# Feed-forward layers on fp16 parts instead of fp32r parts in an attention and FFN kernel

## The chip, the cores and the metric

The kernel runs on one core of one Trainium2 chip. The metric is the device time of one execution in microseconds; the time before is the median of three runs, and one further execution was profiled. Engines are named as in the profile: PE (TensorE, matmuls), PEld (its weight loads), DVE (VectorE), ACT (ScalarE), POOL (GpSimd), SP (SyncE, which only issues DMAs here).

## What is computed

8192 tokens of width 128 go through an attention over 4096 stored keys and values, a residual and a layer norm, then a gated feed-forward network of hidden width 512, a residual and a second layer norm. Everything is fp32.

```python
q = hidden @ Wq.T + bq                            # (8192, 128)
scores = q @ memory_keys.T / sqrt(128)            # (8192, 4096)
mem_out = softmax(scores) @ memory_values
x = layernorm(hidden + mem_out @ Wo.T + bo)

_tlin = lambda x, w, s: einsum('bsi,oi->bso', x, w) * s
h = silu(_tlin(x, w1_w, w1_s)) * _tlin(x, w2_w, w2_s)      # 128 -> 512, twice
h = gelu(_tlin(h, h1_w, h1_s), approximate=False)          # 512 -> 512
h = gelu(_tlin(h, h2_w, h2_s), approximate=False)          # 512 -> 512
out = layernorm(x + _tlin(h, w3_w, w3_s))                  # 512 -> 128
```

The FFN's weight matrices hold -8, 0 and 8 only; their columns' scales are arbitrary fp32 numbers. The kernel finds out on the chip whether the weights are exact in its short format, and has a second path for those that are not.

## The kernel before

**Short formats.** fp32 operands are split into a high part in the format of the matmul and a low part, the rest; a product is then the sum of two or three matmuls in that format. The attention's scores and the whole FFN use fp32r (32 bits wide), probabilities and values use fp16.

**Attention stage** (the first 740 us). Tokens are worked on in 32 pairs of 128-token tiles. One frame (`frame(f, par)` on every engine) has 16 steps t and scores pair f while it ends the softmax of pair f-1 and multiplies the values of pair f-2. TensorE computes three matmuls a step for the scores (L1043 to L1045) and the four of a value step (L1017 to L1022); the values of a pair follow 16 steps behind. VectorE moves each quarter of the scores out of PSUM and takes its maximum (L828), ends each tile with the maximum and the bias of exp (L834, L836), and turns pieces of 32x32 (L795). ScalarE takes exp of a piece at every even step (L629; tile 0 begins at t = 8, right behind the high part of the next q, L608) and makes the fp16 high part of one value step in each t (`high_part`, L638). GpSimd makes the low part behind it (L549). SyncE sends each turned piece with four DMAs (`exchange`, `send`, L380) into one of two buffers `slot_p`, in the order of the pieces; the first send of a pair waits until GpSimd has done the pair before last (`split`).

**The weight check.** In frames 3 to 27 a piece of 226 columns of the packed FFN weights is loaded on ScalarE's queue (t = 3), copied to fp32r (t = 13), subtracted by GpSimd (L555, t = 15), and VectorE reduces the rest's absolute value in the next frame, behind the bias of tile 0 (j = 3, L850). A last maximum, turned on TensorE, gives `low_max`: if it is zero the low parts of the weights are left out.

**The passage** (about 690 to 780 us). `last_values` on TensorE does the values of pairs 30 and 31 with the first layer of block 0 in between (behind value step 8 of pair 30), then h1 of block 0. GpSimd makes the low parts of pair 30 up to step 11, VectorE the later ones and all of pair 31. VectorE also splits x1 of block 0 there (`split_x1(dve, 0)`).

**Feed-forward stage.** 16 blocks of 512 tokens. A turn i (`turn(i, i2, par)`) does on TensorE, in this order: first layer of block i+1 (w1 and w2, 4 chunks, 16 matmuls; chunks 2 and 3 wait for the gate and the product to leave their banks), h2 of block i (32 matmuls, bank j waits for gate or product of block i+1 to leave), h1 of block i+1 (32; behind its chunk 0 the turning of x1 of block i+2), w3 of block i (8). The four banks of `ring` are shared by all. ScalarE: table of Silu, two gates, two high parts, two gates, table of Gelu, two high parts, then for each chunk of h2 and of h1 a Gelu into `gelu` and a second Gelu into `h_hi` (L715, L719). VectorE: products and their low parts, residual and moments of block i+2, its normalisation to x1 (L190), the norm of block i-1, the low parts of h2's Gelus (L895), two of h1's, the split of x1, the last two of h1's. GpSimd: `add_bias` (L158) and `inverse_deviation` (L164, L167), whose rstd VectorE's normalisation waits for. In turn 0 the add for block 3 follows right behind the rstd of block 2.

The order of ScalarE's work at h1's end:

```python
for j in chunks:
    act.wait_ge(done, 4 * b + j + 1)
    at_least(act, gelu_split[layer - 1], 4 * b + j - 3)
    nc.scalar.activation(gelu[:, layer - 1, j, :], ring[:, j, :], ACT.Gelu, ...).then_inc(gelu_f[layer - 1], 1)
    if j == 0:
        at_least(act, *used_by)
    nc.scalar.activation(h_hi[layer][:, j, :], ring[:, j, :], ACT.Gelu, ...).then_inc(gelu_h[layer - 1], 1)
```

## Time and profile before

| | us |
|---|---|
| median of 3 runs | 1117.59 (1116.14 to 1117.80) |
| profiled execution | 1117.46 |
| its span | 1115.50 |
| PE busy | 1079.3 (97%) |
| DVE busy | 972.2 (87%) |
| ACT busy | 903.1 (81%) |
| POOL busy | 643.0 (58%) |
| DMA queue of the sends | 58.7% of 16 engines' time |

The span is what the profiler sees from the first to the last instruction; the rest of the execution's time lies around it. A matmul's busy time is modelled and overlaps its neighbour's: an engine at 97% tells that it hardly stands still, and only the distance from one start to the next tells its pace. In the timelines a row is start, duration, engine, line, operation, output and inputs, shapes, a count of merged instructions, and in brackets the idle time before it with what ended it.

### The profile page before, as it was taken

Reading aid. Unit: us, or ns where it says so; the run is one execution under the profiler, and the core shown is the slowest. Engines: PE = TensorE matmul, PEld = TensorE weight load, DVE = VectorE, ACT = ScalarE, POOL = GpSimd, SP = SyncE. Lnnn points to the kernel's source line nnn. Section 1 sums busy time; section 2 is a strip of 40 time slices with the busy share of each in tenths; the row PEclk is TensorE's granted clock in tenths of the full one; section 3 lists DMA queues with packets and bytes.
Section 4 is the critical chain, followed back from the end, with each engine's and each line's share of the span. In section 5 each row is a group of like instructions: output and inputs, shape, how many; then the busy total and the mean of one; then the engine's idle time right before and its main releaser. Section 6 shows DMA issues by size and latency. Waiting matters only on the chain.

```text
span 1115.5 us, 20017 instructions
## 1 busy us (share of the span) xinstructions
PE 1079.3 (97%) x5324; PEld 770.6 (69%) x5324; DVE 972.2 (87%) x1806; ACT 903.1 (81%) x1609; POOL 643.0 (58%) x617
## 2 busy tenths in 40 slices
PE   6899999999999999999999999979999999999996
PEld 5666666666666666666666666646888888888875
DVE  6999999999999999999999899897888887888884
ACT  6787788878887888888878878788788888888883
POOL 0487888888888888888888888760211211121111
PEclk9999999999999999999999999999999999999998
DMA  6879888988988889888888998891010010011000
GB/s 202 203 185 212 198 201 210 209 200 202 209 203 206 203 207 210 200 202 209 206 203 204 212 200 188 193 255 55 12 46 28 28 56 28 28 35 50 11 13 27
DMA packets 83957, 165.89 MB, mean 149 GB/s; under 512 B 19664, under 2 KB 47824, under 8 KB 83792
## 3 DMA queue, kind: packets, MB, share of 16 engines
q1 hardware_dynamic: 71536, 154.29, 58.7%
q10 hardware_dynamic: 12384, 11.16, 3.5%
q8 instruction: 18, 0.29, 0.1%
q14 instruction: 19, 0.16, 0.0%
HBM read 22.76 MB, written 8.39 MB: 28 GB/s over the span
## 4 chain that ended last, share of the span: by engine, by line
PE 42%; SPq 13%; issue 11%; POOL 10%; ACT 10%; DMA 6%; DVE 5%; ACTq 1%; POOLq 0%; DVEq 0%
PE ring L1090 13%; SPq L380 12%; PE ring L1091 12%; POOL pT L549 10%; DMA slot_p<-rows 6%; ACT rows L629 5%; ACT pT L638 4%; PE o_ps L1017 2%; PE s_ps L1045 2%; PE s_ps L1043 2%; PE s_ps L1044 2%; PE o_ps L1020 2%; PE o_ps L1022 2%; DVE rows L795 2%; DVE rows L828 1%
## 5 line engine op out<-in xcount | busy, mean ns | idle before, releaser
L549 POOL TENSOR_TENSOR pT<-slot_p,pT 128x512 f16<-128x512 f32 x482 | 546.0, 1167 | 124.4 <-ACT pT L638 124.3
L638 ACT ACTIVATE pT<-slot_p 128x512 f16<-128x512 f32 x512 | 296.5, 617 | 73.8 <-DMA slot_p<-rows 68.6
L828 DVE TENSOR_SCALAR_CACHE_REDUCE rows<-s_ps 128x1024 f32<-128x1024 f32 x256 | 309.4, 1209 | 40.5 <-DMA slot_p<-rows 19.9
L795 DVE STREAM_TRANSPOSE rows<-rows 128x1024 f32<-128x1024 f32 x256 | 316.9, 1239 | 5.9 <-issue 4.1
L629 ACT ACTIVATE rows<-rows,bias 128x1024 f32<-128x1024 f32 x256 | 291.6, 1139 | 6.4 <-DVE bias L836 5.9
L1043 PE MATMUL s_ps<-keys,q_buf 128*128 128x512 f32 x512 | 249.2, 487 | 6.8 <-DVE rows L828 3.5
L1017 PE MATMUL o_ps<-pT,v_hi 128*128 128x512 f16 x512 | 197.4, 385 | 13.3 <-POOL pT L549 6.6
L1045 PE MATMUL s_ps<-keys,q_buf 128*128 128x512 f32 x512 | 202.4, 395 | 0.0
L1044 PE MATMUL s_ps<-keys,q_buf 128*128 128x512 f32 x512 | 201.1, 393 | 0.0
L1020 PE MATMUL o_ps<-pT,v_lo 128*128 128x256 f16 x1024 | 196.1, 273 | 0.0
L1022 PE MATMUL o_ps<-pT,v_hi 128*128 128x512 f16 x512 | 194.6, 380 | 0.0
L164 POOL TENSOR_TENSOR var_eps<-moments,eps 128x4 f32<-128x4 f32 x31 | 6.2, 200 | 297.6 <-DVE moments L185 297.6
L1020 PEld LDWEIGHTS o_ps<-pT,v_lo 128*128 128x128 f16 x1024 | 101.1, 99 | 85.4 <-issue 0.6
L1090 PE MATMUL ring<-keys,w_all 128*128 128x512 f32 x384 | 153.4, 400 | 1.0 <-ACT gate L690 0.9
L1091 PE MATMUL ring<-keys,w_all 128*128 128x512 f32 x384 | 150.5, 392 | 0.0
L715 ACT ACTIVATE gelu<-ring,scales 128x512 f32<-128x512 f32 x128 | 87.8, 686 | 57.8 <-PE ring L1091 57.8
L1017 PEld LDWEIGHTS o_ps<-pT,v_hi 128*128 128x128 f16 x512 | 49.3, 96 | 100.0 <-issue 46.8
L1043 PEld LDWEIGHTS s_ps<-keys,q_buf 128*128 128x128 f32 x512 | 96.8, 189 | 25.7 <-DVE rows L828 4.9
L1045 PEld LDWEIGHTS s_ps<-keys,q_buf 128*128 128x128 f32 x512 | 96.1, 188 | 22.5
L1044 PEld LDWEIGHTS s_ps<-keys,q_buf 128*128 128x128 f32 x512 | 96.8, 189 | 17.3
L895 DVE TENSOR_TENSOR h_lo<-gelu,h_hi 128x512 fp32r<-128x512 f32 x128 | 81.9, 686 | 25.5 <-ACT h_hi L719 25.4
L1090 PE MATMUL ring<-h_hi,w_all 128*128 128x512 f32 x256 | 103.1, 403 | 0.3 <-ACT gate L690 0.3
(110 smaller groups left out, 1329.2 us busy)
## 6 DMA issues: line engine op xcount, KB each, us to landing
slot_p<-rows SPq DMA_DIRECT2D x1024, 128.0 KB, 3.0
x_in<-in_x SPq DMA_DIRECT2D x16, 256.0 KB, 3.4
x_in<-in_xT ACTq DMA_DIRECT2D x30, 128.0 KB, 3.3
out<-y_out SPq DMA_DIRECT2D x15, 256.0 KB, 2.4
o_scratch<-o_sum ACTq DMA_DIRECT2D x29, 128.0 KB, 2.7
o_in<-o_scratch SPq DMA_DIRECT2D x14, 256.0 KB, 3.1
z<-in_w_all ACTq DMA_DIRECT2D x25, 113.0 KB, 2.7
rows<-in_w_all SPq DMA_DIRECT2D x1, 2816.0 KB, 12.1
```

The lines of the kernel that those rows point to most:

```text
L549: nc.gpsimd.tensor_tensor(halves(s % RING, 1), slots_first(pp, s), halves(s % RING, 0), ALU.subtract).then_inc(split, 1)
L629: nc.scalar.activation(s, s, ACT.Exp, bias=bias[:, tile:tile + 1], scale=SCALE, accum_out=den[:, bass.ds((2 * p + tile) * PIECES + k, 1)]) ...
L638: nc.scalar.activation(halves(s % RING, 0), slots_first(pp, s), ACT.Copy).then_inc(highed, 1)
L795: nc.vector.transpose(row_piece(tile, k), row_piece(tile, k)).then_inc(turned, 1)
L828: nc.vector.tensor_scalar(row_piece(tile, k), s_ps[:, j % 2, :], 1.0, None, ALU.mult, ALU.max, accum_out=part_max[:, tile, k:k + 1]).then_ ...
L1017: nc.tensor.matmul(o_ps[:, pp, :], v_hi[:, 2 * s, :], pT[:, s % RING, 0, :], start=s == 0, stop=False, skip_group_check=True)
L1020: nc.tensor.matmul(o_ps[:, pp, 0:2 * P], v_lo[:, 2 * s + c, :], pT[:, s % RING, c, 0:2 * P], start=False, stop=False, skip_group_check=True)
L1043: nc.tensor.matmul(out, q_h, k_h, start=True, stop=False)
L1044: nc.tensor.matmul(out, q_h, k_l, start=False, stop=False)
L1045: last = nc.tensor.matmul(out, q_l, k_h, start=False, stop=True)
L1090: nc.tensor.matmul(out, wh, hh, start=n == 0, stop=False)
L1091: last = nc.tensor.matmul(out, wh, hl, start=False, stop=final and not low_weights)
```

## The change

- The first three FFN layers (w1 and w2, h1, h2) multiply fp16 high and low parts with fp16 weights; w3 stays fp32r, with a copy of its weights made on ScalarE. The number of matmuls is the same.
- To stay in fp16's range, h is scaled by powers of two. They come from bounds that are found on the chip: the largest weight of each layer and the largest scale (`find_maxima`, `turn_maxima`, `spread_maxima`, `share_maxima`, `keep_maxima`, `set_scales`).
- h1's high part is no longer a second Gelu from PSUM but a Copy of the first one, scaled (`gelu_high`), and it is queued one chunk behind the Gelus; the low part is a fused multiply and subtract. TensorE's first layer and h2's bank now wait for the first Gelu (`gelu_f`), not for the high part.
- The check takes 256 columns a frame instead of 226. VectorE reduces rest and weights in one instruction (512 columns) at j = 2 instead of j = 3; the load is issued at t = 9 instead of t = 3.
- Inexact weights no longer get low parts: the raw weights are kept in fp32, and whole fp32 matmuls are run. h2's raw weights are scaled by GpSimd in turn 0, on either path. Their load waits for the last scores instead of the last sends.

The diff, cut to its core:

```diff
-CHECK_COLS = 226
+CHECK_COLS = 256
-        self.w_all = sb("w_all", [P, CHECK_COLS * CHECKS], FP32R)
+        self.w_all = sb("w_all", [P, CHECK_COLS * CHECKS], FP16)
+        self.w3_hi = sb("w3_hi", [P, HC * P], FP32R)
...
+    def find_maxima(self, dve, parts):
+        by_chunk = parts[:, :].rearrange("p (c n) -> p n c", n=2)
+        self.nc.vector.reduce_max(self.found[:, 0:1], by_chunk[:, 1, :], AX.X).then_inc(self.found_ready, 1)
...
+    def spread_maxima(self, dve):
+        dve.wait_ge(self.found_turned, 1)
+        self.nc.vector.reduce_max(self.low_max[:, :], self.x1_ps[0:FOUND, 2 * P:3 * P], AX.X).then_inc(self.low_found, 1)
+        dve.wait_ge(self.low_found, 1)
+        self.nc.vector.tensor_scalar(self.spread[:, :], self.ident[0:FOUND, :], 0.0, self.low_max[:, :], ALU.mult, ALU.add).then_inc(self.low_spread, 1)
...
+    def set_scales(self, dve):
+        dve.wait_ge(self.bounding, 1)
+        self.nc.vector.tensor_tensor(self.sizes[:, :], self.maxima[:, 1:4], self.maxima[:, 4:7], ALU.mult).then_inc(self.bounding, 1)
+        dve.wait_ge(self.bounding, 2)
+        self.nc.vector.tensor_scalar(self.bounds[:, 0:1], self.sizes[:, 0:1], self.sizes[:, 1:2], LEAST, ALU.mult, ALU.max).then_inc(self.bounding, 1)
...
+        self.nc.vector.tensor_scalar(self.powers[:, :].bitcast(I32), self.bounds[:, :].bitcast(I32), EXPONENT, None,
+                                     ALU.bitwise_and).then_inc(self.bounding, 1)
+        dve.wait_ge(self.bounding, 5)
+        self.nc.vector.reciprocal(self.inverses[:, :], self.powers[:, :]).then_inc(self.bounding, 1)
+        dve.wait_ge(self.bounding, 6)
+        for col, by, factor in ((HC, self.inverses[:, 0:1], 1.0), (2 * HC, self.powers[:, 0:1], 1.0), (3 * HC, self.powers[:, 1:2], 2.0 ** 9)):
+            self.nc.vector.tensor_scalar(self.scales[:, col:col + HC], self.scales[:, col:col + HC], by, factor,
+                                         ALU.mult, ALU.mult).then_inc(self.scales_set, 1)
...
-        for tile in range(2):
-            for k in range(PIECES):
-                sp.wait_ge(sent[tile][k], 16 * GROUPS * PAIRS)
+        sp.wait_ge(scored, 8 * PAIRS)
         sp.dma_start(raw, w_raw[:, 0:W_COLS]).then_inc(raw_loaded, 16)
...
         def turn(i, i2, par):
             if valid(i + 2, BLOCKS):
                 stage.add_bias(pool, i + 2, i2 + 1, par)
                 stage.inverse_deviation(pool, i + 2, 0)
+            if is_step(i, 0):
+                pool.wait_ge(raw_loaded, 16)
+                pool.wait_ge(stage.scales_set, 4)
+                nc.gpsimd.tensor_tensor(raw_h2, raw_h2, stage.h1_scale[:, :].broadcast_to([P, HC * HID]), ALU.mult).then_inc(raw_scaled, 1)
...
-                if t == 3 and checking(f):
-                    at_least(act, w_rested, f - FIRST_CHECK)
+                if t == 9 and checking(f):
+                    at_least(act, w_maxed, f - FIRST_CHECK)
                     act.dma_start(w_check, w_raw[:, bass.ds((f - FIRST_CHECK) * CHECK_COLS, CHECK_COLS)]).then_inc(check_loaded, 16)
...
+        def gelu_high(b, j):
+            act.wait_ge(gelu_f[0], 4 * b + j + 1)
+            nc.scalar.activation(h_hi[1][:, j, :], gelu[:, 0, j, :], ACT.Copy, scale=stage.h1_scale[:, :]).then_inc(gelu_h[0], 1)
...
             if valid(i + 1, BLOCKS):
-                gelus(i + 1, 1, mid1_done, (mid2_done, 4 * (i + 1)), (1, 2, 3))
+                gelu_high(i + 1, 0)
+                for j in (1, 2, 3):
+                    mid1_of(i + 1, j)
+                    if j >= 2:
+                        gelu_high(i + 1, j - 1)
+                gelu_high(i + 1, 3)
...
+        nc.scalar.activation(stage.w3_hi[:, :], stage.w_all[:, W_AT["w3"]:W_COLS], ACT.Copy).then_inc(stage.w3_ready, 1)
...
-                if j == 3 and checking(f - 1):
+                if j == 2 and checking(f - 1):
                     dve.wait_ge(w_rested, f - FIRST_CHECK)
-                    nc.vector.reduce_max(low_parts[:, bass.ds(f - FIRST_CHECK - 1, 1)], w_rest, AX.X,
+                    nc.vector.reduce_max(low_parts[:, bass.ds((f - FIRST_CHECK - 1) * 2, 2)],
+                                         check_room.rearrange("p (n c) -> p n c", n=2), AX.X,
                                          apply_absolute_value=True).then_inc(w_maxed, 1)
...
+            if layer == 1:
+                nc.vector.scalar_tensor_tensor(out=h_lo[1][:, j, :], in0=gelu[:, 0, j, :], scalar=stage.h1_scale[:, :],
+                                               in1=h_hi[1][:, j, :], op0=ALU.mult, op1=ALU.subtract).then_inc(gelu_split[0], 1)
...
         stage.output_sum(dve, PAIRS - 3, 1)
+        stage.set_scales(dve)
         stage.split_x1(dve, 0)
```

## Rows read from the trace of the kernel before

**Rows 1.** Busy us (x instructions) of PE, PEld, DVE, ACT, POOL; PEclk, DMA, GB/s.
```profile
100.00:700.00 600.00, 595.99 (x3059) 400.89 (x3058) 554.42 (x848) 497.38 (x933) 502.56 (x458) 1.00 0.88 204
790.00:1100.00 310.00, 309.07 (x1418) 250.68 (x1418) 251.06 (x680) 254.71 (x409) 49.44 (x68) 1.00 0.10 31
```
**Rows 2.** Timeline of ACT in one turn: start us, duration, instruction, [idle before <-releaser].
```profile
876.88 0.69 ACT L715 ACTIVATE gelu<-ring,scales 128x512 f32<-128x512 f32 x1 [0.54 <-PE ring L1091]
878.16 1.28 ACT L684 ACT_TABLE_LOAD   x1
885.02 1.14 ACT L698 ACTIVATE keys<-gate 128x512 fp32r<-128x512 f32 x2
886.07 0.67 ACT L715 ACTIVATE gelu<-ring,scales 128x512 f32<-128x512 f32 x1
...
898.62 0.69 ACT L715 ACTIVATE gelu<-ring,scales 128x512 f32<-128x512 f32 x1 [0.54 <-PE ring L1091]
```
**Rows 3.** Waits of SyncE's queue in 100 to 700 us: total, times, longest.
```profile
SPq L380 <- POOL pT L549: 39.9, 24, 2.2
```
**Rows 4.** Timelines of DVE, ACT, POOL and PE in frames 18 and 19.
```profile
420.82 0.39 DVE L850 TENSOR_REDUCE low_parts<-z 128x226 f32 x1
442.97 0.39 DVE L850 TENSOR_REDUCE low_parts<-z 128x226 f32 x1
421.03 1.15 ACT L629 ACTIVATE rows<-rows,bias 128x1024 f32<-128x1024 f32 x1
443.60 1.14 ACT L629 ACTIVATE rows<-rows,bias 128x1024 f32<-128x1024 f32 x1
409.59 1.17 POOL L549 TENSOR_TENSOR pT<-slot_p,pT 128x512 f16<-128x512 f32 x1 [0.50 <-ACT pT L638]
411.16 0.38 PE L1017 MATMUL o_ps<-pT,v_hi 128*128 128x512 f16 x1
433.62 0.10 PEld L1017 LDWEIGHTS o_ps<-pT,v_hi 128*128 128x128 f16 x1 [0.61 <-POOL pT L549]
```
**Rows 5.** Timeline of PE in the attention stage, one period of two steps.
```profile
401.22 0.40 PE L1044 MATMUL s_ps<-keys,q_buf 128*128 128x512 f32 x1
...
402.38 0.39 PE L1017 MATMUL o_ps<-pT,v_hi 128*128 128x512 f16 x1
...
403.92 0.40 PE L1044 MATMUL s_ps<-keys,q_buf 128*128 128x512 f32 x1
```
**Rows 6.** Timelines of ACT and PE in turn 0: last Gelu of h1, start of h2.
```profile
767.98 0.69 ACT L715 ACTIVATE gelu<-ring,scales 128x512 f32<-128x512 f32 x1 [0.55 <-PE ring L1091]
774.08 0.50 PE L1090 MATMUL ring<-h_hi,w_all 128*128 128x512 f32 x1 [0.25 <-ACT gate L690]
```
**Rows 7.** Timeline of PE in the turn of rows 2: start of h2, turning of x1.
```profile
883.08 0.50 PE L1090 MATMUL ring<-h_hi,w_all 128*128 128x512 f32 x1
...
892.51 0.27 PE L231 MATMUL x_ps<-ident,x 128*128 128x128 f32 x1
```
**Rows 8.** Timelines of DVE, POOL and PE around x1, in a full turn and in turn 0.
```profile
890.81 1.12 DVE L190 TENSOR_SCALAR x<-z,moments,rstd 128x128 f32<-128x128 f32 x4 [0.29 <-POOL rstd L167]
781.68 1.30 POOL L158 TENSOR_TENSOR xb<-x_in,bo_all 128x512 f32<-128x512 f32 x1
781.81 1.25 DVE L190 TENSOR_SCALAR x<-z,moments,rstd 128x128 f32<-128x128 f32 x1 [1.48 <-POOL rstd L167]
782.98 0.85 DVE L190 TENSOR_SCALAR x<-z,moments,rstd 128x128 f32<-128x128 f32 x3
783.88 0.33 PE L231 MATMUL x_ps<-ident,x 128*128 128x128 f32 x1 [0.24 <-DVE x L190]
```
**Rows 9.** Groups by line, 100 to 700 us: busy us, mean ns | idle before.
```profile
L549 POOL TENSOR_TENSOR pT<-slot_p,pT 128x512 f16<-128x512 f32 x430 | 487.0, 1167 | 96.9 <-ACT pT L638 96.9
...
L836 DVE TENSOR_SCALAR bias<-row_max 128x1 f32<-128x1 f32 x53 | 8.2, 154 | 1.8
```
**Rows 10.** Timeline of POOL in the passage, beside the same subtraction on DVE.
```profile
738.32 1.61 POOL L568 TENSOR_TENSOR pT<-slot_p,pT 128x512 f16<-128x512 f32 x1
```

More of the change, by code:

```diff
@@ L769, in _ @@
         stage.output_half(act, PAIRS - 1, 1)
-        gelus(0, 1, mid1_done, (mid2_done, 0))
+        act.wait_ge(stage.scales_set, 4)
+        for j in range(HC):
+            mid1_of(0, j)
+            gelu_high(0, j)
         turns(act, turn)
@@ L1079, in frame, with split_products @@
                     stage.turn_x1(pe, 0)
         frames(pe, frame)
[L1083 to L1086 removed]
+        def split_products(out, pairs, sem_done, parts_ready=None):
+            for n, (w, hh, hl) in enumerate(pairs):
                 if parts_ready:
                     pe.wait_ge(parts_ready[0], parts_ready[1] + n + 1)
[L1089 to L1094 removed]
@@ L1096, in layer @@
-        def layer(out, name, j, src, sem_done, low_weights, width=HID, parts_ready=None):
-            split_products(out, [(weight(name, k, j, width), weight_low(name, k, j, width),
-                                  h_hi[src][:, k, :], h_lo[src][:, k, :]) for k in range(HC)], sem_done, low_weights,
-                           parts_ready if j == 0 else None)
+                nc.tensor.matmul(out, w, hh, start=n == 0, stop=False)
+                last = nc.tensor.matmul(out, w, hl, start=False, stop=n == len(pairs) - 1)
@@ new lines, in split_products, with whole_products, layer @@
+            last.then_inc(sem_done, 1)
+        def whole_products(out, pairs, sem_done, parts_ready=None):
+            for n, (w, h) in enumerate(pairs):
+                if parts_ready:
+                    pe.wait_ge(parts_ready[0], parts_ready[1] + n + 1)
+                last = nc.tensor.matmul(out, w, h, start=n == 0, stop=n == len(pairs) - 1)
+            last.then_inc(sem_done, 1)
+        def layer(out, b, name, j, src, sem_done, low_weights, width=HID, parts_ready=None):
+            parts_ready = parts_ready if j == 0 else None
+            if low_weights:
+                whole_products(out, [(raw_weight(name, k, j, width), gelu[:, src - 1, k, :] if src else product(b, k))
+                                     for k in range(HC)], sem_done, parts_ready)
+            else:
+                split_products(out, [(weight(name, k, j, width), h_hi[src][:, k, :], h_lo[src][:, k, :])
+                                     for k in range(HC)], sem_done, parts_ready)
```

185 lines of the change are left out of this document (102 added, 83 removed).

## Prediction

> **What bounds the kernel now.** I read the busy time by stage first. In the attention stage TensorE is busy 596 of 600 us, in the feed-forward stage 309 of 310 us, always at the full clock [rows 1]; those busy times are modelled ends, so next comes the spacing of the matmuls and what is late next. In the feed-forward stage a turn (one block of 512 tokens) takes 21.74 us, from the last Gelu behind h1 to the same one a turn later [rows 2]. TensorE hardly waits there, so only its pace counts, until another chain becomes longer. In the attention stage a second loop is as long: ScalarE's exp, GpSimd's low parts, SyncE's sends (which wait for GpSimd 24 times in 27 frames [rows 3]), and back to TensorE, which is found waiting 0.61 us for GpSimd at the start of a pair [rows 4].
>
> **1. The pace of a matmul.** Six fp32r matmuls and six equivalents in fp16 take 2.70 us; five intervals of fp32r take 1.16 us, 0.232 each, which leaves 0.218 for fp16 [rows 5]. So fp16 is worth 0.014 us on each 512-column matmul. A block has 88; the 8 of w3 stay fp32r. 80 x 0.014 = 1.1 us a block, 18 us in 16 blocks, if TensorE stays the limit. The number of matmuls is unchanged.
>
> **2. ScalarE behind the last h1 product.** Before, two operations stand between the end of h1's chunk 3 and the loading of the Silu table, both Gelus (876.88 to 878.16, 1.28 us) [rows 2]. After, there are three: the Gelu, the high part of chunk 2 (now queued behind it), the high part of chunk 3. The extra one is a Copy from SBUF; two of them take 1.05 us before the next operation starts, 0.52 each [rows 2], and the last one is a little shorter than a Gelu: +0.46. Behind it are queued the table, the gates (on which VectorE's products wait, and h2 on TensorE, which needs gate 2 to leave bank 0), and the second pair of high parts, on which VectorE's low parts and then the normalised x1 wait. What this chain takes is seen in turn 0, where TensorE does wait for it: 774.08 - 767.98 = 6.10 us from Gelu to h2 [rows 6]; in a full turn it is 883.08 - 876.88 = 6.20 [rows 2, 7]. So it has 0.10 us of slack. New: 6.56.
> From h2's start 40 matmuls (h2 and h1's first chunk) come in 40 x 0.218 = 8.72 us: 15.28 after the Gelu. There TensorE turns x1, which VectorE finishes at 890.81 + 1.12 = 891.93, 15.05 after the Gelu [rows 8]; with ScalarE's 0.46 and a signal of 0.05 that is 15.56, the later of the two. From the turning to the next last Gelu it was 898.62 - 892.51 = 6.11 [rows 2, 7], now less 24 x 0.014: 5.77. Sum 21.33 against 21.74: 0.4 us a turn instead of 1.1. Over the 14 full turns -5.6 us. Bounds: 0 (a Copy scaled from a register column as slow as a Gelu, and a late split of x1) and -1.1 a turn. VectorE's fused low part of h1 may cost 0.06 more than the plain subtraction, four times a turn; it fits in VectorE's idle fifth [rows 1]. In the last turn the extra operation and the two fused ones delay z2 by some 0.8 where h2 gains 0.45; block 0 gains 0.3 in h1. These cancel.
>
> **3. The weights of h2, scaled on GpSimd in turn 0.** This runs whatever the weights are. It has 2048 columns: four times the add of 512 columns there is 5.2 us [rows 8], four times the subtraction to fp16 4.7 [rows 9]; I take 4.7. It is issued right behind the rstd of block 2, on which VectorE's x1 waits too. The trace shows what comes of that: at 781.68 GpSimd's add starts, at 781.81 VectorE's first normalisation, which takes 1.25 us where the next three take 0.85 together, and its successor starts at 782.98, when GpSimd is done; TensorE waits for x1 then [rows 8]. Such operations take turns and do not overlap: where both engines subtract back to back GpSimd's last 1.61 instead of 1.17 us [rows 9, 10]. So with the scaling in that place VectorE's first slice ends at about 786.7, then the add takes its turn (some 1.1) before the other three slices (0.85): x1 is ready at about 788.5 instead of 783.83. That is +4.7 on TensorE, which has no slack there; less 0.3 of faster h1: +4.4. Bounds: 0 (VectorE gets in first) and +5.5.
>
> **4. The weight check in the attention loop.** The reduction grows from 226 to 512 columns: 0.39 us [rows 4] for 226, by the same rate at most 0.88, by one column a ns 0.68; I take 0.64 in sequence. It moves from behind the bias of tile 0 to before chunk 3 of it, so that bias comes 0.64 later. The slack of bias to the exp that reads it is about 0.2 us in one frame (the reduction behind it starts at 420.82, exp at 421.03) and 0.6 in the next (442.97, 443.60) [rows 4]; exp is late by 0.45 and by 0 to 0.1 in turn. Queued behind it on ScalarE are the high parts of the last steps of a pair, which release GpSimd's, which release the sends of the next pair, which run back to back and let TensorE's values start. This loop spans two frames. The one that holds TensorE back (0.61) is that with little delay; in the other GpSimd ends at 409.59 + 1.17 = 410.76 what TensorE starts at 411.16 [rows 4], 0.4 of slack for 0.45 of delay. So some 0.15 per two frames, and up to 0.07 a frame for GpSimd's 256 columns instead of 226: 0.08 to 0.15 a frame, +2.0 us over 25 frames with what is passed on. Bounds: 0, and 0.54 per two frames, +6.8. The load at step 9 instead of 3 has four steps to land, 5.4 us by [rows 5]; a transfer of its size needs some 3 us of them, so nothing.
> In the last frames exp waits for the bias itself, so the last wide reduction, the four small maxima and the spreading of the maxima pass through: +0.5, +0.4, +0.3, together +1.2 (0 to +3), estimates from the 0.39 us reduction and the 0.154 us operation [rows 4, 9].
>
> **5. set_scales.** Ten small VectorE operations ahead of the split of x1, 0.154 us each [rows 9] and about 0.04 for the signal: 1.9 us. TensorE's first layer follows some 3 us behind the old split, and GpSimd keeps TensorE back later: hidden. But GpSimd subtracts back to back there. If the five of more than one column each have to let it pass, 1.1 us apiece, the split comes about 3 us too late, of which some 1 is absorbed: +2.2. Bounds 0 and +3; I take +1.5. The Trainium skill (VectorE: DVE Perf Modes, section on mode 2×_2P) lets single-source fp32 operations in SBUF take both read ports if their outer dimension is even, which four columns are and one is not. Here one column ran in 0.154 us beside a busy GpSimd; for four no row shows it; by the page this term would be 2.2 and the sum 1121.7.
> The copy of w3 on ScalarE (+0.6) lies in ScalarE's wait for the first layer. The raw load, now issued without waiting for the sends to land, keeps its place in SyncE's queue, and nobody reads it before turn 0.
>
> **Sum.** Profiled run 1117.46 us (span 1115.50 and 1.96 around it; the median is 1117.59): -5.6 + 4.4 + 2.0 + 1.2 + 1.5 = +3.5, so 1121.0, own range 1117.5 to 1125.
>
> **Rivals.** (a) TensorE's pace decides: the extra Copy and x1 find slack that I do not see, all 18 us come, less parts 3 to 5 (9.1): 1108.5. Against it: turn 0, where the chain is seen at 6.10. Chance 0.12. (b) The long scaling costs nothing (VectorE gets in first, or GpSimd takes it in pieces): 1116.6. Against it: the slice of 1.25 us. 0.20. (c) Slower: the exp delay decides the attention loop. Place: the bias of tile 0 in frames 3 to 27; price 0.54 us per two frames; it decides as soon as the delayed loop has no slack left, which I put at 0.4: +6.8 instead of 2.0, and the last frames and set_scales at their upper ends (+3.3): 1129. For it: TensorE waits for GpSimd now. 0.15. (d) The change does not do what it says: the weights are found inexact and whole fp32 matmuls run. Their values are 0 and 8 in size and exact in fp16, so 0.02; the time would be far above the range. My forecast keeps 0.51.
>
> **Chances.** A measurement can tell about 0.2%, 2.2 us, from no change. Slower by more (over 1119.8): 0.68 of the forecast, (c), (d): 0.52. Within: 0.3 of the forecast and most of (b): 0.27. Faster: (a), a third of (b): 0.21. The range that leaves 2 in 10 out is 1111 to 1128; it holds cases of both signs, and the likeliest one's own is 1117.5 to 1125.
>
> **What would show it.** Turns of 21.3 us, fp16 matmuls at 0.218, the table load 1.74 us behind the last h1 Gelu, and TensorE waiting for gate 2 and for x1: part 2. Turns of 20.6: (a). A GpSimd operation of over 4 us in turn 0 and a VectorE slice as long beside it: part 3. Longer waits of TensorE for GpSimd at a pair's start: part 4, and (c) if every second frame grows by half a us. A split of x1 that TensorE waits for: part 5. I am wrong if x1's chain is not the later one in a turn, or if exp waits for bias in neither frame.

## The result, and the profile after

| | before | after |
|---|---|---|
| median us | 1116.88 (1116.14 to 1117.80, 4 runs) | 1129.51 (1129.19 to 1129.69, 4 runs) |
| ratio, 95% interval | | 1.0112 (1.0095 to 1.0130) |
| span of the profiled execution | 1115.5 | 1127.4 |

The change makes the kernel slower by 12.6 us. The sign was forecast, the size was not: 1121.0 was said, with 1111 to 1128 as the range, and the time is 1.5 us above it.

I cut both spans at operations of ScalarE that both kernels have: the copy of the last q (in the middle of frame 30), the load of the Gelu table behind the gates in turn 0, and the same in turn 1. Timeline of ScalarE, after (start us, duration, instruction, idle before and what ended it):

```profile
695.84 0.48 ACT L664 ACTIVATE q_buf<-x_ps,bq_col 128x256 fp32r<-128x256 f32 x1 [1.21 <-PE x_ps L1077]
...
783.62 1.28 ACT L740 ACT_TABLE_LOAD   x1
...
810.98 1.28 ACT L740 ACT_TABLE_LOAD   x1
```

Before, these stood at 689.93, 774.62 and 796.67. So:

| stretch | before | after | difference | forecast |
|---|---|---|---|---|
| attention, to the last q | 689.93 | 695.84 | +5.9 | +2.9 (part 4) |
| passage, to the table load of turn 0 | 84.69 | 87.78 | +3.1 | +1.8 (part 5, and 0.3 of part 4) |
| turn 0 to turn 1 | 22.05 | 27.36 | +5.3 | +4.4 (part 3) |
| the rest | 318.83 | 316.42 | -2.4 | -5.6 (part 2) |
| sum | 1115.50 | 1127.40 | +11.9 | +3.5 |

The 0.3 is the spreading of the maxima, which stands behind the last q (716.81 to 723.19). No stretch has the wrong sign, and all four miss in the same direction. Each column is one profile. Three more profiles with this same attention stage were taken in the experiments; their last q stands at 696.49, 697.61 and 697.88, so the stage lost between 5.9 and 8.0 us, and differences of 1 or 2 us in it are told by medians only.

Busy time by stage, answering [rows 1]; the columns are those of rows 1:

```profile
100.00:700.00 600.00, 592.01 (x3033) 397.46 (x3032) 550.98 (x843) 494.05 (x927) 498.36 (x454) 1.00 0.87 203
790.00:1100.00 310.00, 299.67 (x1407) 146.26 (x1406) 257.12 (x675) 256.27 (x409) 53.50 (x69) 0.99 0.10 30
```

The fp16 weight loads show at once (PEld 146 us instead of 251). They overlap the matmuls in both kernels; whether part of the shorter spacing is theirs, no run tells. TensorE's busy time fell by 9.4 us in the feed-forward stage and by 4 in the attention stage, where nothing of its work was changed. There it stood still, which is what a lower busy time means on the engine that sets the pace.

**A turn.** Timelines of ScalarE and TensorE in a full turn, answering [rows 2, 7, 8]:

```profile
884.18 0.66 PE L296 MATMUL x_ps<-ident,x 128*128 128x128 f32 x4
890.06 0.69 ACT L772 ACTIVATE gelu<-ring,scales 128x512 f32<-128x512 f32 x1 [0.43 <-PE ring L1172]
890.64 1.32 ACT L778 ACTIVATE h_hi<-gelu,h_scale 128x512 f16<-128x512 f32 x2
891.99 1.28 ACT L740 ACT_TABLE_LOAD   x1
```

The table load comes 1.93 us behind the last Gelu of h1, where it came 1.28 behind it [rows 2] and 1.74 was forecast. The two scaled Copies take 1.32 together and 0.71 singly, the plain ones 1.14 together [rows 2] and 0.62 singly; the estimate counted 0.52 for the extra one, half of the 1.05 from the start of two plain ones to the next operation. Turns take 21.61 us.

**Turn 0.** Timelines of GpSimd, VectorE and TensorE, answering the last four of [rows 8]:

```profile
789.68 1.02 POOL L180 TENSOR_TENSOR rstd<-var_eps,minus_half 128x4 f32<-128x4 f32 x1
790.67 3.60 POOL L644 TENSOR_TENSOR raw<-raw,h_scale 128x2048 f32<-128x2048 f32 x1
794.23 1.26 POOL L171 TENSOR_TENSOR xb<-x_in,bo_all 128x512 f32<-128x512 f32 x1
790.80 5.28 DVE L203 TENSOR_SCALAR x<-z,moments,rstd 128x128 f32<-128x128 f32 x4 [1.48 <-POOL rstd L180]
796.14 0.66 PE L296 MATMUL x_ps<-ident,x 128*128 128x128 f32 x4 [4.25 <-DVE x L203]
796.92 0.63 PE L1172 MATMUL ring<-in_room,w_all 128*128 128x512 f16 x1
...
799.48 0.63 PE L1172 MATMUL ring<-in_room,w_all 128*128 128x512 f16 x1
...
800.26 0.38 PE L1172 MATMUL ring<-in_room,w_all 128*128 128x512 f16 x1
```

The slices of x1 stand behind the scaling and then behind the add, as forecast; TensorE waits 4.25 us. What was not forecast is behind it: the seven matmuls from 796.92 to 799.48 start 0.43 us apart, not 0.22. The granted clock of the stretch says why (0.72 is the mean of stretches at half and at the full level, that is 1.2 and 2.4 GHz), with the stretch behind it:

```profile
795.00:801.00 6.00, 4.86 (x17) 2.15 (x18) 4.15 (x8) 1.89 (x3) 0.48 (x1) 0.72 0.00 0
801.00:811.00 10.00, 9.75 (x48) 5.13 (x47) 6.45 (x10) 8.28 (x14) 0.00 (x0) 1.00 0.00 1
```

**The passage.** Timelines of VectorE and TensorE; the forecast had no row for the operations on four columns beside a busy GpSimd. There are nine operations (the prediction counted ten):

```profile
740.49 0.75 DVE L269 TENSOR_TENSOR sizes<-maxima 128x3 f32<-128x3 f32 x1
741.27 0.21 DVE L271 TENSOR_SCALAR bounds<-sizes 128x1 f32<-128x1 f32 x1
...
741.77 0.58 DVE L275 TENSOR_SCALAR powers<-bounds 128x2 int32<-128x2 int32 x1
742.39 0.17 DVE L278 RECIPROCAL inverses<-powers 128x2 f32<-128x2 f32 x1
742.59 0.88 DVE L281 TENSOR_SCALAR scales<-scales,inverses 128x4 f32<-128x4 f32 x1
743.38 2.30 DVE L281 TENSOR_SCALAR scales<-scales,powers 128x4 f32<-128x4 f32 x2
745.60 0.14 DVE L283 TENSOR_SCALAR h_scale<-inverses 128x1 f32<-128x1 f32 x1
745.66 1.39 DVE L229 CAST x_hi<-rows 128x512 f16<-128x512 f32 x1
747.92 0.38 PE L1171 MATMUL ring<-x_hi,w_all 128*128 128x512 f16 x1 [3.59 <-DVE x_lo L231]
```

The nine take 5.2 us (740.49 to 745.66), five of them more than half a microsecond, and TensorE waits 3.59 us for the split of x1. Its first matmuls behind the wait still come at full pace; from 749.00 to 752.41 they are at half the clock again.

**The attention loop.** ScalarE's exp waits for the bias hardly at all: the waits of 100 to 690 us, answering [rows 3, 4] (engine, line, waited for: us in total, times, longest):

```profile
ACT pT L694 <- DMA slot_p<-rows: 60.1, 25, 3.1
...
PE o_ps L1098 <- POOL pT L611: 7.9, 15, 0.7
...
ACT rows L685 <- DVE bias L911: 2.0, 3, 0.9
```

The same of the kernel before:

```profile
ACT pT L638 <- DMA slot_p<-rows: 59.4, 26, 3.2
...
PE o_ps L1017 <- POOL pT L549: 3.2, 10, 0.6
```

TensorE waits for GpSimd at a pair's start 7.9 us, before 3.2. The frames are longer by nearly what rival (c) had said, but its mechanism, exp behind a late bias, isn't there. The experiments had to find what is.

### The profile page after: what moved, and what is told of

It is laid out like the page before. It is cut to its first block, busy times and chain, and to the rows that moved or that the text cites. A ratio compares the mean times of both kernels' runs of the same rounds, so it can differ in the third digit from the quotient of the medians.

```text
span 1127.4 us, 20029 instructions
## 1 busy us (share of the span) xinstructions
PE 1073.1 (95%) x5326; PEld 656.6 (58%) x5326; DVE 981.8 (87%) x1820; ACT 907.2 (80%) x1610; POOL 645.2 (57%) x617
## 4 chain that ended last, share of the span: by engine, by line
issue 33%; PE 20%; POOL 18%; ACT 9%; DVE 7%; SPq 6%; DMA 4%; ACTq 0%; POOLq 0%; DVEq 0%
POOL pT L611 15%; SPq L446 5%; DMA slot_p<-rows 4%; ACT rows L685 3%; ACT pT L694 3%; PE ring L1171 3%; PE ring L1172 2%; PE o_ps L1098 2%; PE s_ps L1126 2%; PE s_ps L1124 2%; PE s_ps L1125 2%; PE o_ps L1101 2%; PE o_ps L1103 2%; DVE rows L870 2%; POOL rstd L180 1%
## 5 line engine op out<-in xcount | busy, mean ns | idle before, releaser
L1171 PE MATMUL ring<-in_room,w_all 128*128 128x512 f16 x256 | 98.1, 383 | 0.0
L1172 PE MATMUL ring<-in_room,w_all 128*128 128x512 f16 x256 | 98.1, 383 | 0.0
L1171 PE MATMUL ring<-h_hi,w_all 128*128 128x512 f16 x256 | 97.3, 380 | 0.4 <-ACT gate L748 0.4
L1172 PE MATMUL ring<-h_lo,w_all 128*128 128x512 f16 x256 | 97.1, 379 | 0.0
```

The source lines that it names most:

```text
L1171: nc.tensor.matmul(out, w, hh, start=n == 0, stop=False)
L1172: last = nc.tensor.matmul(out, w, hl, start=False, stop=n == len(pairs) - 1)
```

## Experiments

All times are medians beside runs of the kernel before on the same chip (1117.3 to 1117.5). The changed kernel itself, 1129.5, was measured beside 1116.9, so a gain against it is uncertain by that half a us, beside the spread of the runs.

### Turn 0: the scaling of the raw weights

```diff
-            if is_step(i, 0):
-                pool.wait_ge(raw_loaded, 16)
-                pool.wait_ge(stage.scales_set, 4)
-                nc.gpsimd.tensor_tensor(raw_h2, raw_h2, ..., ALU.mult).then_inc(raw_scaled, 1)
```

> The changed kernel without GpSimd's scaling of h2's raw weights in turn 0 (nothing on the path of exact weights reads them, so the result is whole; the path for inexact weights is left without its scaled weights). My theory: the scaling (3.60 us on GpSimd) and VectorE's first slice of x1 beside it (3.55 us) are one wait in two records, and TensorE's 4.25 us wait for x1 behind them also costs the full clock for some 5 us afterwards. Then turn 0 (from h1's last Gelu of block 0 to that of block 1) falls from 26.89 us to about 20.2 (before: 20.24), TensorE's wait for x is under 0.5 us, the matmuls behind it keep their spacing of 0.22 us, and the time is 1129.5 - 6.6 = 1122.9. Rival: only the wait goes and turn 0 is held by ScalarE's extra Copies as well: 1125 to 1126, turn 0 near 23. Rival: the transfer of the raw weights or another queue is behind it: no change.

Measured: 1123.95 us (ratio 1.0057, 1.0044 to 1.0070). From table load to table load turn 0 takes 22.38 us instead of 27.36: 5.0 us, and the median falls by 5.6. VectorE's four slices and TensorE's wait, without the scaling:

```profile
792.55 1.99 DVE L203 TENSOR_SCALAR x<-z,moments,rstd 128x128 f32<-128x128 f32 x4 [1.48 <-POOL rstd L180]
794.60 0.66 PE L296 MATMUL x_ps<-ident,x 128*128 128x128 f32 x4 [0.96 <-DVE x L203]
796.00:806.00 10.00, 9.75 (x47) 4.98 (x46) 6.84 (x12) 7.71 (x13) 0.00 (x0) 1.00 0.00 1
```

From the last Gelu of block 0's h1 to that of block 1 it is 21.91 us, in the kernel before 790.03 - 767.98 = 22.05. (The 20.24 that was expected here as the time before ends at the Gelu one chunk earlier, so the forecast of 20.2 and of 1122.9 asked too much.) Turn 0 is back where it was.

The wait falls by 3.3 us and the clock stays full behind it. Eight intervals at half pace (796.92 to 800.26, 3.34 us) would have been 1.73 at 0.216: 1.6 us. 3.3 + 1.6 = 4.9 of the 5.0. So about a third of what the scaling costs is the clock. The theory holds. The wait left over, 0.96 instead of under 0.5, doesn't come from a late x1: it is turned 16.04 us behind the last Gelu, before 15.90. TensorE gets there sooner, by some 0.6 us on 40 fp16 matmuls.

### The passage: where the scales are set

```diff
-        stage.set_scales(dve)
         stage.split_x1(dve, 0)
         for s in range(LATE_STEP, STEPS):
             low_part(PAIRS - 2, 0, s)
+        stage.set_scales(dve)
```

> The changed kernel with the ten small VectorE operations that set the scales put behind the low parts of pair 30's values instead of ahead of the split of x1 of block 0. Theory: in their old place four of them wait for GpSimd's subtractions (0.58 to 1.2 us instead of 0.15), 5.2 us in all, so the split comes late, TensorE waits 3.59 us for it, and its matmuls come at half the pace for a few us afterwards. Behind the values GpSimd is idle: the ten take some 2 us, TensorE waits under 0.7 us at its first layer, the time from frame 30's q projection to the end of pair 30's values falls from 60.9 to 57.5, and the time is 1129.5 - 3.4 = 1126.1. Rival: the split itself (1.39 + 0.69 us) and the low parts behind it are what is late, and the scales' 2 us now delay the products instead: a gain of under 1.5 us. Rival: what is gained there is lost again, since VectorE's low parts of pair 31 set the pace of the passage: same time.

Measured: 1127.01 us (ratio 1.0091, 1.0078 to 1.0104), 2.5 us better. The same operations behind the low parts:

```profile
749.68 1.10 DVE L269 TENSOR_TENSOR sizes<-maxima 128x3 f32<-128x3 f32 x1
...
751.72 0.23 DVE L281 TENSOR_SCALAR scales<-scales,inverses 128x4 f32<-128x4 f32 x1
...
757.60 0.39 PE L1098 MATMUL o_ps<-pT,v_hi 128*128 128x512 f16 x1 [1.15 <-DVE pT L875]
```

On four columns an operation takes 0.23 us with GpSimd idle and 0.88 to 1.2 beside it. The first of the nine still met GpSimd's last subtraction (1.10). By the Trainium skill (SBUF — State Buffer, section on who interferes with whom) a VectorE operation with two inputs in SBUF, or one in a two-port mode, contends with GpSimd, and a reduction on trn2 never does. The trace agrees at every row: `sizes` (two inputs, 0.75 and 1.10) and the four-column scalings were held up, the reciprocal on two columns (0.17) and the one-column operations (0.14 to 0.21) were not, and the check's reduction takes 0.68 us wherever it stands.

From the last q to the end of pair 30's values the time falls from 60.24 to 56.67 us, 3.6 as expected (before: 56.64). Part is given back: the products and the low parts of pair 31 behind them come later, TensorE waits 1.15 us at 757.60, and from there to the end of pair 31's values it takes 15.2 instead of 13.8 us, which leaves 2.2 of the 3.6. So the first theory and the second rival are both true in part.

### The turns: order of the high parts

```diff
                 for j in (1, 2, 3):
                     mid1_of(i + 1, j)
-                    if j >= 2:
-                        gelu_high(i + 1, j - 1)
-                gelu_high(i + 1, 3)
+                    gelu_high(i + 1, j)
```

> The changed kernel with h1's high part of chunk 2 made ahead of the Gelu of chunk 3 instead of behind it (the last four operations of ScalarE in a turn are Gelu 2, high 2, Gelu 3, high 3 instead of Gelu 2, high 1, Gelu 3, high 2, high 3). Theory: the third operation behind h1's last product is what took the gain away: a scaled Copy starts its successor 0.61 us later. With it out of the way the gates, and with them high parts, products, low parts and x1, come 0.6 us earlier and a turn takes 21.0 us instead of 21.61; 14 turns give 8.5 us: 1121. Rival: TensorE's pace is what is left: a turn can't be under 20.6, so up to 1115.5. Rival: VectorE's chain to x1 (residual, moments, GpSimd's rstd, normalisation) and not ScalarE decides the turn: 21.6 and 1129.

Measured: 1122.43 us (ratio 1.0040, 1.0028 to 1.0052), 7.1 us better. Timeline of ScalarE:

```profile
847.08 0.69 ACT L772 ACTIVATE gelu<-ring,scales 128x512 f32<-128x512 f32 x1 [0.29 <-PE ring L1170]
847.80 0.72 ACT L778 ACTIVATE h_hi<-gelu,h_scale 128x512 f16<-128x512 f32 x1
848.54 1.28 ACT L740 ACT_TABLE_LOAD   x1
```

The table load is 1.46 us behind the last Gelu instead of 1.93, 0.47 earlier, and a turn takes 21.15 us instead of 21.61, 0.46 shorter. What leaves ScalarE's end of the turn comes off the turn one for one, so the chain that begins there sets it, and neither TensorE's pace nor a chain that passes ScalarE by. The 0.6 that was expected is 0.47, because a high part right behind its own Gelu waits for that Gelu to end (0.72 from start to start instead of 0.58). The 20.6 us that TensorE's pace would allow (21.74 less 1.1) are still not reached. In this profile the slow matmuls behind the 4.26 us wait of turn 0 last 6.8 us instead of 3.4; turn 0 takes 28.19 us, and the median need not have that.

### The attention loop

First the reduction, put back behind the bias in the changed kernel, and put forward in the kernel before.

```diff
-                if j == 2 and checking(f - 1):
+                if j == 3 and checking(f - 1):
```

> The changed kernel with VectorE's reduction of the weight check put back behind the bias of tile 0 (j = 3 instead of j = 2); its length (512 columns) and the load at step 9 stay. Theory (the rival (c) of the prediction): the reduction in front of the bias delays every exp of tile 0, and the attention loop, which has no slack, pays 0.4 to 0.5 us in two frames. Then exp's wait for the bias falls from 7.6 us to 5.9 or less, two frames take 44.55 us instead of 44.95 as before the change, the attention stage is 5 to 6 us shorter, and the time is 1124. Rival: the length of the reduction or GpSimd's 256 columns are what the loop pays for, wherever the reduction stands: 1129, frames unchanged. Rival: the load at step 9 (with its wait for the reduction, now later, in front of ScalarE's work of step 9) is the cost: 1129 or slower.

Measured: 1128.43 us (ratio 1.0102, 1.0089 to 1.0115); 22 frames take 496.3 us as in the changed kernel (496.3 to 499.2 in the four profiles of its attention stage). The 5 to 6 us of the theory, the prediction's own, aren't there; the 1.1 us of median are hardly clear of the noise.

```diff
-                if j == 3 and checking(f - 1):
+                if j == 2 and checking(f - 1):
```

> The kernel before with one part of the change alone: VectorE's reduction of the weight check (226 columns as before) at j = 2, ahead of the bias of tile 0, instead of j = 3. If its place costs the attention loop (the prediction's exp delay, 0.39 us here), every second frame is 0.2 to 0.4 us longer than the 22.5 us of before and the time is 1120 to 1122. If the place is free, as putting it back in the changed kernel suggests (1128.4 against 1129.5), the time is 1117.3 and the frames stay at 22.08 and 22.5.

Measured: 1117.46 us against 1117.40 (ratio 1.0004, 0.9995 to 1.0013). Alone, with 226 columns, the place is free. Next the load, in the kernel before:

```diff
-                if t == 3 and checking(f):
+                if t == 9 and checking(f):
                     at_least(act, w_rested, f - FIRST_CHECK)
                     act.dma_start(w_check, ...).then_inc(check_loaded, 16)
```

> The kernel before with another part of the change alone: the load of the weight check (113 KB) issued on ScalarE's queue at step 9 instead of step 3. Theory: the DMA engines are 88% busy in the attention stage, the last sends of a pair land while ScalarE waits for them (2.5 us in every second frame before, 2.9 after), and the load at step 9 falls in front of just these sends, where at step 3 it lay under others; then frames take 22.9 to 23.0 us every second time instead of 22.5, and the time is 1121 to 1123. Rival: the load's size and place do not matter (its 1.9 us in the trace are within the sends' noise): 1117.3, and the cause is the wider work of VectorE, GpSimd and ScalarE.

Measured: 1121.76 us (ratio 1.0044, 1.0031 to 1.0058). One load of 113 KB a frame, issued six steps later, costs 4.4 us. Nobody waits for the load itself. ScalarE waits longer for sends (59.4 before) and TensorE for GpSimd (3.2 before), in 100 to 690 us:

```profile
ACT pT L638 <- DMA slot_p<-rows: 65.8, 25, 3.2
...
PE o_ps L1017 <- POOL pT L549: 7.1, 18, 0.8
```

The traces also tell which sends the load meets. A pair has eight pieces of four DMAs each. Means over pairs 6 to 27, in us from the issue of a piece's first DMA to the landing of its last:

| kernel | load at step | pieces 1, 2 | pieces 3 to 6 | piece 7 | piece 8 | first issue to last landing |
|---|---|---|---|---|---|---|
| before | 3 | 4.23 | 5.00 | 5.60 | 5.34 | 23.32 |
| before, load late | 9 | 4.23 | 4.34 | 6.24 | 5.82 | 23.88 |
| changed | 9 | 4.24 | 4.35 | 5.96 | 5.54 | 23.61 |
| changed, load early | 3 | 4.24 | 5.00 | 5.49 | 5.27 | 23.29 |

At step 3 the load is issued behind the second piece, and the next four take 0.7 us longer; at step 9 it is issued behind the sixth, and the last two, the slowest anyway, take 0.6 and 0.5 longer. Most sends land sooner with the late load and the kernel is slower all the same, so it must be the last two that cost.

> The kernel before, its check load at step 3 as it was, and one more, small load (8 columns, 4 KB) issued on ScalarE's queue at step 9 in frames 3 to 27, into a tensor that nothing reads. If it is the bytes of a load at step 9 that hold up the last sends of a pair, this costs nothing: 1117.4. If it is the issuing of one (0.34 us on ScalarE's queue, or 128 more packets among the sends'), it costs as much as the whole load did: 1121 to 1122.

```diff
+                if t == 9 and checking(f):
+                    at_least(act, tiny_loaded, 16 * (f - FIRST_CHECK))
+                    act.dma_start(tiny[:, :], w_raw[:, 0:8]).then_inc(tiny_loaded, 16)
```

Measured: 1116.36 us against 1117.45 (ratio 0.9991, 0.9982 to 1.0000): no cost. It is the bytes, not the issuing.

> The changed kernel with 226 columns a frame in the weight check instead of 256 (all engines: load, copy, subtraction, reduction of 452 instead of 512 columns); place of the reduction and time of the load as in the changed kernel. The borders of the layers are missed by some columns in the bounds; since every layer's largest weight is the same here the bounds, and all results, are the same. If the size is what the attention loop pays for (GpSimd's subtraction, the load), the frames go back to 22.5 and the time falls to 1124 to 1126. If place or time of the load is the cause: 1129.

```diff
-CHECK_COLS = 256
+CHECK_COLS = 226
```

Measured: 1127.47 us (ratio 1.0095, 1.0079 to 1.0110), 2.0 us better, between the theory and its rival and hardly clear of the intervals. The 22 frames, 496.0 us, are just under the 496.3 to 499.2 of the four profiles with 256 columns. The size is a small part, which these runs don't tell well from none.

> The changed kernel with the check's load back at step 3. So that it can be issued there, the piece of the weights lies in two rooms by turns (a new tensor of 512 columns beside the old one); the reduction of 512 columns stays at j = 2. Theory: the place of the load is the attention loop's cost, 4.4 us in the kernel before (1121.8 against 1117.4), and its size (256 columns instead of 226) about 1 more: every second frame goes back from 22.9 to 22.5 or 22.6 us and the time is 1129.5 - 4.4 = 1125.1. Rival: once the other work is wider too (reduction, subtraction, copy), these set the loop and the load's place gives less than 1.5 us: 1128 or more.

```diff
+    rooms = (check_room, sb("check_more", [P, 2 * CHECK_COLS], FP32)[:, :])
...
-                if t == 9 and checking(f):
-                    at_least(act, w_maxed, f - FIRST_CHECK)
-                    act.dma_start(w_check, ...)
+                if t == 3 and checking(f):
+                    at_least(act, w_rested, f - FIRST_CHECK)
+                    act.dma_start(w_check[par], ...)
```

Measured: 1128.30 us (ratio 1.0102, 1.0087 to 1.0118). This was a miss: 4.4 expected, 1.2 gained, as the rival had it. Its trace shows why. Timelines of VectorE and ScalarE in frame 19, the kernel before first:

```profile
416.80 1.23 DVE L828 TENSOR_SCALAR_CACHE_REDUCE rows<-s_ps 128x1024 f32<-128x1024 f32 x1 [0.61 <-DMA slot_p<-rows]
...
420.69 0.15 DVE L836 TENSOR_SCALAR bias<-row_max 128x1 f32<-128x1 f32 x1
```

The changed kernel (load at step 9, reduction ahead of the bias):

```profile
419.78 1.22 DVE L903 TENSOR_SCALAR_CACHE_REDUCE rows<-s_ps 128x1024 f32<-128x1024 f32 x1
...
420.93 0.68 DVE L925 TENSOR_REDUCE low_parts<-z 128x512 f32 x1
...
424.11 0.15 DVE L911 TENSOR_SCALAR bias<-row_max 128x1 f32<-128x1 f32 x1
...
424.70 1.14 ACT L685 ACTIVATE rows<-rows,bias 128x1024 f32<-128x1024 f32 x1
```

The changed kernel with the load at step 3:

```profile
419.83 1.23 DVE L904 TENSOR_SCALAR_CACHE_REDUCE rows<-s_ps 128x1024 f32<-128x1024 f32 x1 [1.18 <-DMA slot_p<-rows]
...
420.98 0.68 DVE L926 TENSOR_REDUCE low_parts<-check_more 128x512 f32 x1
...
424.16 0.15 DVE L912 TENSOR_SCALAR bias<-row_max 128x1 f32<-128x1 f32 x1
...
424.44 1.15 ACT L686 ACTIVATE rows<-rows,bias 128x1024 f32<-128x1024 f32 x1 [0.75 <-DVE bias L912]
```

And its waits in 100 to 690 us, 10.6 us of exp for the bias instead of 2.0:

```profile
ACT rows L686 <- DVE bias L912: 10.6, 19, 1.1
```

A load of 113 to 128 KB lies among sends that keep the DMA engines 87 to 89% busy. At step 3 it holds up the third piece, and VectorE's third move of tile 0's scores waits for a send; VectorE then has no room for 0.68 us more ahead of the bias, and exp is late. At step 9 it spares that move and holds up the last sends of a pair, which ScalarE's first high part waits for. Means over frames 6 to 27, in us from ScalarE's copy of q to the start named (that of the third move lies ahead of it):

| kernel | load, reduction | third move | exp | first high part | 22 frames |
|---|---|---|---|---|---|
| before | 3, j = 3 | -4.04 | 0.40 | 9.05 | 491.4 |
| before, reduction forward | 3, j = 2 | -4.03 | 0.43 | 9.05 | 491.1 |
| before, load late | 9, j = 3 | -4.54 | 0.37 | 9.31 | 496.2 |
| changed | 9, j = 2 | -4.55 | 0.37 | 9.17 | 496.3 |
| changed, reduction back | 9, j = 3 | -4.54 | 0.37 | 9.15 | 496.3 |
| changed, load early | 3, j = 2 | -3.80 | 0.83 | 9.26 | 495.6 |

The prediction's exp delay (0.45 forecast, 0.83 - 0.40 = 0.43 here) is real where the load is early, and covered where it is late. The change swapped one delay for the other. If so, only both edits together bring the gain. (The early load came with a second room for the piece of weights, which no run has by itself; in the kernel before, the load alone cost its 4.4 us in one room.)

By the Trainium skill (DMA: Bandwidth & Descriptors, section on queues, rings and completion order) a DMA engine takes packets of its queues in turn, so a load on ScalarE's queue slows sends on SyncE's while both have work. The load at step 9 (+4.4 us), the pieces that are slow behind it at either step, and the 4 KB load (-1.1, at the edge of the noise) agree with that; no view here shows the engines' order itself.

### All together

The edits above in one kernel, the scaling on GpSimd inside a branch that only inexact weights take, in three forms of the check.

Load at step 9, reduction at j = 3:

> The changed kernel with the four single edits together: h2's raw weights scaled only where the weights are inexact (a branch on GpSimd ahead of the turns), the scales set behind the low parts of pair 30's values, the reduction of the check behind the bias, and h1's high parts each right behind its Gelu. If the costs lie one behind the other, as the theory has it, the gains add up: 1129.5 - 5.6 - 2.5 - 1.1 - 7.1 = 1113.2, under the kernel before (1117.3). Rival: two of them share a slack (the scales' place and turn 0's start, or the turns' chain that VectorE takes over once ScalarE is faster): 1116 to 1118.

Measured: 1115.89 us (ratio 0.9985, 0.9976 to 0.9994), 2.7 us above the sum of the single gains. Passage (85.60 us), turn 0 (21.91) and the rest (309.27) have theirs; the attention stage, 698.02 us to the last q, is no better than in the changed kernel's own profiles (695.84 to 697.88). So the 1.1 us of the reduction's place didn't come; what the other 1.6 are is not shown.

Load at step 3, reduction at j = 2:

> The changed kernel with the four edits that stand for a cost each: the check's load at step 3 into two rooms by turns, h2's raw weights scaled only where the weights are inexact, the scales set behind pair 30's low parts, h1's high parts right behind their Gelus. The reduction of the check keeps its place of the changed kernel (j = 2). If the costs add up: 1129.5 - 4.4 - 5.6 - 2.5 - 7.1 = 1109.9; by the sum that the version with the late load gave (1115.9 with the reduction behind the bias), 1111.5. Rival: the passage or the turns hide the attention's gain, which nothing in the traces suggests: 1115.9.

Measured: 1113.60 us (ratio 0.9970, 0.9958 to 0.9982), 2.3 us under the version with the late load and the reduction behind the bias, where 4.4 was expected; exp starts 0.67 us behind the copy of q, so the early reduction still costs.

Load at step 3, reduction at j = 3:

> The version with all four edits (load at step 3 into two rooms by turns, conditional scaling, scales behind pair 30's low parts, high parts in order) and the reduction of the check behind the bias as well. Theory: with the load at step 3 the send of tile 0's third piece lands later, VectorE's move of the scores waits 0.4 to 0.8 us for it, and only then a reduction of 0.68 us in front of the bias makes exp late (0.25 and 0.75 us in two frames that follow each other); with the load at step 9 VectorE is 0.7 us ahead there, which is why putting the reduction back alone gave nothing. So here, and not in the kernel with the late load, it brings the frames from 22.45 to 22.33 us on average as before the change (491.5 us for 22 frames instead of 493.9), and the time to 1111.1. Rival: the loop is held by the wider subtraction and copy on GpSimd and ScalarE, not by exp: 1113.6.

Measured: 1109.73 us (ratio 0.9925, 0.9911 to 0.9940), against 1117.38 for the kernel before: faster than both kernels. Cut as above, its stretches are 691.76, 85.07, 21.90 and 309.27 us: the first three are within 2 us of the kernel before, and the rest is 9.6 us shorter. That is what the fp16 matmuls give once the costs are out of the way. A turn takes 21.13 us. Here the reduction's place is worth 3.9 us and the load's 6.2, where in the changed kernel they were worth 1.1 and 1.2 singly. The means are those of the kernel before again (third move -4.04, exp 0.39, first high part 9.07). Waits of 100 to 690 us:

```profile
ACT pT L700 <- DMA slot_p<-rows: 59.2, 26, 3.3
...
PE o_ps L1102 <- POOL pT L612: 3.5, 10, 0.7
...
ACT rows L691 <- DVE bias L915: 0.5, 2, 0.3
```

TensorE's wait for GpSimd is back at 3.5 us (before 3.2, changed 7.9). The 22 frames were 492.9 us, 1.0 less than with the early reduction, where 2.4 was expected; about as much again lies in the last three frames (68.3 against 69.4) and in the passage (85.07 against 86.01). Single profiles of kernels with the same attention stage differ by up to 3 us in the 22 frames, so for the total the medians decide; the two edits' sum there (1.1 + 6.2) lies within the 5.9 to 8.0 us that the stage had lost, and is no finer than the intervals.

## Why the prediction was off, step by step

**Part 1, the pace.** Right. fp16 matmuls start 0.216 to 0.217 us apart (0.218 forecast), and TensorE has slack in a turn.

**Part 2, the turn.** The mechanism was right, the size off. The chain over ScalarE, gates, products and x1 is the one that counts, and x1 is the later end of it. From the last Gelu (890.06 - 21.61 = 868.45) to the turning of x1 at 884.18 it is 15.73 us (15.56 forecast), from there to the next last Gelu 5.88 (5.77). The term that was mis-sized is the extra operation: 0.65 us (1.93 - 1.28) instead of 0.46. A Copy with a scale from a register column was priced as a plain one; the upper bound named for it, "as slow as a Gelu", was the better guess. The new high part takes 0.62 us to the start of the next, and a Gelu 0.57. The gain is 0.13 us a turn instead of 0.4: 1.8 instead of 5.6 in 14 turns, and 2.4 for the whole rest. With so long a chain, 0.27 us of estimate is two thirds of the gain.

**Part 3, turn 0.** The mechanism was right in every row, and the scaling cheaper than forecast (3.60 instead of 4.7 us). It still cost more in all, 5.0 us by the experiment instead of 4.4, since TensorE ran at half its clock behind the wait, 1.6 us. The wait itself came out at 3.3 us more, not 4.7. The prediction let every stall cost its own length and no more.

**Part 4, the attention loop.** This is the step whose mechanism failed. It put the load's new place at nothing: it asked one question, whether the load lands in time (it does, in 2.7 us), and not whose transfers it delays. That alone is worth 4.4 us in the kernel before, where the last two pieces of a pair take 0.6 and 0.5 us longer. The exp delay, on which the sum rested, was hidden in the changed kernel by the same move. Rival (c) came near in price (5.9 for 22 frames; 4.9 in this profile, up to 7.8 in others of the same stage) and even nearer in time (1129), and was wrong in cause: that is luck. The test that the prediction named for (c), every second frame longer by half a us, came true and proved nothing about it; the wait of exp for the bias, also named, was the row that told.

**Part 5, set_scales.** Priced at +1.5, between 0 and +3; it was 3.6 up to the end of pair 30's values, of which the edit gave back 2.2 in the passage and 2.5 in the median. The suspects were the right ones: the products of three columns, the powers of two and the three scalings of four, five operations, waited for GpSimd; the sixth with more than one column, the reciprocal on two, did not. The measured rows are 0.88 and 1.15 (half of 2.30) against 0.23. By the Trainium skill's page that the prediction cited (VectorE: DVE Perf Modes, section on mode 2×_2P) four columns can take both ports; the trace agrees, and its 2.2 was nearer than the 1.5 taken. What it missed: the cast of the split waits too (1.39 instead of 0.70), and again TensorE's clock falls behind its 3.59 us wait.

**The sum.** The four misses are 3.0 (attention), 1.3 (passage), 0.9 (turn 0) and 3.2 (turns), 8.4 us, all on one side. The largest is a mis-sized term, the extra operation; the attention's is the one with a wrong mechanism, and either alone would have stayed inside the range. Each part's own bounds held its stretch, the passage only just. The values taken inside the bounds were the cheaper ones each time, and a sum of four such choices leaves the range even if each of them is plausible.

What is still open: whether the 2 us of the narrow check are its size or noise, and why the reduction's place, free or worth 1 us with the late load, is worth 3.9 with the early one when the 22 frames of those two profiles differ by 1.0 only. A load at other steps wasn't tried.

## What to carry to other kernels

Where DMA engines are near 90% busy, moving a transfer is moving a cost: ask which sends it now lies among and who waits for them, not only whether it arrives in time. A wait that vanished from one place may be hiding a second one, so test two suspects together as well as singly: here each edit alone gave about 1 us, and with the other one in place it gave 4 and 6. And price an added stall of the tensor engine with the slow matmuls behind it.

## What the runs showed of the hardware

- From 0.6 and 1.1 us behind waits of 4.25 and 3.59 us, TensorE's 512-column fp16 matmuls started 0.43 us apart for 3.4 us, at the 1.2 GHz level, before they came back to 0.216. The granted clock fell to that level too behind a wait of 3.39 us that both kernels have (from 729.5 us on before) and behind one of 2.26 (without the scaling, in the passage), and in some profiles it stayed there for 6.8 us. Behind a wait of 0.96 us it didn't, but once, at 122 us with the reduction put back, it fell behind two waits of 0.95 and 0.84 us that followed each other. By the Trainium skill (TensorE: Matmul & The Clock Gate, part 1) a TensorE that has been idle is at half its clock; the rows agree that waits bring it there.
- A GpSimd multiply of 128x2048 fp32 with a broadcast column takes 3.60 us, less than three of its 512-column adds (1.26 each).
- ScalarE: a Copy of 128x512 from SBUF with its scale from a column of SBUF takes 0.71 us, a plain one 0.62; two of them 1.32 and 1.14.
- DMA: with the engines 87 to 89% busy, a 113 KB load among the sends made the four 512 KB pieces issued behind it 0.4 to 1.0 us slower at one place, and the two behind it 0.5 and 0.6 at another; a 4 KB one cost nothing.
- VectorE: 0.23 us for a scaling of four columns alone, 0.88 to 1.2 beside GpSimd's back-to-back subtractions; one column 0.14 to 0.21 beside them; a reduction of 512 columns 0.68 us at either place.
